# Writing out the loops of a fused state-space and codebook kernel, and finding the best code with two maxima

## The reference

```python
x = x + mamba(group_norm(x))     # layer norm, projection to 2 x 1024, causal convolution of 4 taps,
                                 # silu, selective scan with 16 states, gate, projection to 512
xf = group_norm(x)               # tokens x 512
xn = xf / norm(xf);  mn = m / norm(m)            # m: 1024 codes x 512
score = xn @ mn.T                                # 8192 x 1024
idx = argmax(score, axis=1)
counts = segment_sum(ones, idx);  esum = segment_sum(xf, idx)
new_m = m * 0.999 + esum / (counts[:, None] + 1e-6) * 0.001
x = x + softmax(score, axis=1) @ new_m
```

## Time and profile before

| | before |
|---|---|
| median of 3 runs | 4800.43 us (4799.78 to 4807.43) |
| span of the profiled execution | 4805.1 us |
| TensorE busy | 4532.6 us, 94% |
| VectorE busy | 4100.0 us, 85% |
| ScalarE, GpSimd busy | 2967.6 us, 3361.6 us |

### The profile page before, as it was taken

How to read it: one execution, slowest core, us unless ns; L and a number is a source line. 1 busy time by engine, 2 the same in 40 slices (tenths; PEclk the granted TensorE clock), 3 DMA queues, 4 the chain that set the end, 5 groups by cost and what they waited for, 6 DMA issues and landing times. The chain is left out here.

```text
span 4805.1 us, 115630 instructions
## 1 busy us (share of the span) xinstructions
PE 4532.6 (94%) x47164; PEld 2985.2 (62%) x47164; DVE 4100.0 (85%) x4361; ACT 2967.6 (62%) x6018; POOL 3361.6 (70%) x1679
## 2 busy tenths in 40 slices
PE   6999899995899999999999999999999899999999
PEld 5666666663455555555555555555554688888787
DVE  6888898877999999999999999999997667777332
ACT  2666666665777777777777777777765445453211
POOL 0666676664999999999999999999997222222000
PEclk9999999997999999999999999999999999999999
DMA  4345434335233323332333323332332111111543
GB/s 170 134 157 176 159 129 152 130 143 177 71 100 101 101 80 101 98 98 86 93 98 98 98 86 99 103 99 81 99 100 80 68 55 77 79 79 79 201 201 140
DMA packets 195543, 538.02 MB, mean 112 GB/s; under 512 B 15904, under 2 KB 15920, under 8 KB 186016
## 3 DMA queue, kind: packets, MB, share of 16 engines
q1 hardware_dynamic: 190144, 482.41, 30.4%
q0 software_dynamic: 4960, 49.25, 2.6%
HBM read 329.22 MB, written 202.38 MB: 111 GB/s over the span
## 5 line engine op out<-in xcount | busy, mean ns | idle before, releaser
L1040 POOL TENSOR_TENSOR sc_hc<-sc_hc,sc_c_rep 128x1024 f32<-128x1024 f32 x1024 | 2387.6, 2374 | 124.5 <-ACT sc_state L1053 94.7
L1235 DVE TENSOR_TENSOR_SCAN sc_hc<-l_m,sc_state,sc_ring 128x512 f32<-128x512 f32 x2048 | 2419.1, 1257 | 11.7 <-PE sc_ring L1162 7.1
L1085 ACT ACTIVATE l_m<-l1s_v,l_neg_a 128x512 f32<-128x512 f32 x2048 | 1351.4, 707 | 8.0 <-DMA l1s_v<-spill 7.7
L1162 PEld LDWEIGHTS sc_ring<-sc_diag,l1s_iota 64*64 64x64 f32 x32768 | 896.4, 133 | 459.4 <-issue 453.4
L1162 PE MATMUL sc_ring<-sc_diag,l1s_iota 64*64 64x128 f32 x32768 | 1040.8, 274 | 45.9 <-DVE sc_hc L1235 42.9
L1172 PE MATMUL sc_y_ps<-sc_hc,sc_fold 128*64 128x512 f32 x4096 | 935.4, 599 | 0.9 <-POOL sc_hc L1040 0.9
L1053 ACT ACTIVATE sc_state<-sc_hc 128x2 f32<-128x2 f32 x1024 | 207.2, 202 | 625.1 <-DVE sc_hc L1235 624.9
L1172 PEld LDWEIGHTS sc_y_ps<-sc_hc,sc_fold 128*64 128x64 f32 x4096 | 271.4, 137 | 484.0 <-issue 461.7
L1505 POOL TENSOR_TENSOR l_count<-l_count,as_oh 128x1024 f32<-128x1024 f32 x64 | 182.4, 2850 | 506.5 <-DVE as_oh L1699 506.5
L923 PE MATMUL sc_o_ps<-l_et,l_sums 128*128 128x512 f32 x960 | 464.0, 606 | 4.4 <-ACT sc_b_col L1063 4.4
L71 PE MATMUL fr_mm<-fr_xn_hi,l0f_w_in_hi 128*128 128x512 f32 x1024 | 437.0, 427 | 27.1 <-DVE fr_delta L708 11.8
(11 more groups left out here) (194 smaller groups left out, 6427.4 us busy)
## 6 DMA issues: line engine op xcount, KB each, us to landing
sc_duz<-spill SPq DMA_DIRECT2D x128, 768.0 KB, 6.0
l1s_v<-spill SPq DMA_DIRECT2D x256, 256.0 KB, 4.0
spill<-fr_z SPq DMA_DIRECT2D x64, 512.0 KB, 2.8
spill<-fr_u SPq DMA_DIRECT2D x32, 1024.0 KB, 10.0
spill<-fr_du SPq DMA_DIRECT2D x32, 1024.0 KB, 4.3
spill<-fr_delta SPq DMA_DIRECT2D x32, 1024.0 KB, 6.5
sc_c_rep<-bc SPq DMA_DIRECT2D x128, 256.0 KB, 4.5
soft<-l_et SPq DMA_DIRECT2D x16, 2048.0 KB, 6.2
```

The costliest lines, as they stand in the source:

```text
L1040: nc.gpsimd.tensor_tensor(hc[:, p], hc[:, p], c_rep[:, 2 * q:2 * q + 2, :], ALU.mult).then_inc(s_hp, 1)
L1085: nc.scalar.activation(da[:, p % 4, r, :], delta[:, i % 2, p % 2, :], ACT.Exp, scale=keep.neg_a[:, c:c + 1]).then_inc(s_da, 1)
L1162: done = nc.tensor.matmul(to[:, :, k::4], dut[rows, i % 2, k, HALF * h:HALF * h + HALF], diag[rows, u, 4 * q + c:4 * q + 4:2, k, :], start ...
L1235: nc.vector.tensor_tensor_scan(hc[:, p, r, :], da[:, p % 4, r, :], ring[:, SLOT[at], r::2], state[:, i, 2 * p + r:2 * p + r + 1], ALU.mult ...
```

## The change

The loops of `front`, `assign` and `readout` become Python loops, so that every pass is written out with constants for its waits and addresses. In `nearest` the index of the best code is found in another way: `iota` now counts down from 1024 to 1, `e` is used for a while to hold `iota` where the score equals the largest and 0 elsewhere, and a second maximum over `e` gives the highest such value, `near`. The one-hot row compares `iota` with it. `exp` waits for that second maximum, since it overwrites `e`.

```diff
-                with eng.Fori(1 - b, NJ - 1) as j:
+                for j in range(1 - b, NJ - 1):
                     main(b, j, lambda n: (b, j + n), False)
...
-                with eng.Fori(head, NJ // 2 - 1) as i:
+                for i in range(head, NJ // 2 - 1):
                     pair(b, i, False)
...
             def exp(g, s):
                 act.wait_ge(s_nb, TT * g + s + 1)
-                act.wait_ge(s_ix, TT * g + s + 1)
+                act.wait_ge(s_if, TT * g + s + 1)
...
                 dve.wait_ge(s_top, n + 1)
-                nc.vector.memset(idxf[:, s:s + 1], 0.0)
-                nc.vector.max_index(idx[:, s, :], top[:, s, :], sc_ps[:, s % 2, :]).then_inc(s_ix, 1)
+                nc.vector.memset(near[:, s, :], 0.0)
+                dve.wait_ge(s_tt, 2 * TT * g + 2 * s + 2 * TT - 2)
+                nc.vector.scalar_tensor_tensor(e[:, s % 2, :], sc_ps[:, s % 2, :], top[:, s, 0:1], keep.iota[:], ALU.is_equal,
+                                               ALU.mult).then_inc(s_ix, 1)
...
                 dve.wait_ge(s_ix, n + 1)
-                nc.vector.tensor_copy(idxf[:, s:s + 1], idx[:, s, 0:1]).then_inc(s_if, 1)
+                nc.vector.max(near[:, s, :], e[:, s % 2, :]).then_inc(s_if, 1)
...
-                nc.vector.tensor_scalar(oh[:, u, s, :], keep.iota[:], idxf[:, s:s + 1], None, ALU.is_equal).then_inc(s_oh, 1)
+                nc.vector.tensor_scalar(oh[:, u, s, :], keep.iota[:], near[:, s, 0:1], None, ALU.is_equal).then_inc(s_oh, 1)
...
-            with pool.Fori(1, NG // 2) as i:
+            for i in range(1, NG // 2):
...
-                with sp.Fori(0, NJ // 2) as i:
+                for i in range(0, NJ // 2):
...
-            with dve.Fori(0, NG // 2 - 1) as i:
+            for i in range(0, NG // 2 - 1):
...
-        "iota": np.arange(KM, dtype=np.float32)[None, :],
+        "iota": np.arange(KM, 0, -1, dtype=np.float32)[None, :],
```

More of the change, by code:

```diff
@@ L23 @@
 F32R = mybir.dt.float32r
-U32 = mybir.dt.uint32
 ALU = mybir.AluOpType
@@ L1405, in assign @@
         nb = w.sb("nb", [P, TT])
-        idx = w.sb("idx", [P, TT, 8], U32)
-        idxf = w.sb("idxf", [P, TT])
+        near = w.sb("near", [P, TT, 8])
         oh = w.sb("oh", [P, 2, TT, KM], F32R)
@@ L1779, in chunks @@
             body(1, 1, 0)
-            with eng.Fori(1, NG // 2) as i:
+            for i in range(1, NG // 2):
                 for u in range(2):
```

## The result

| | before | changed |
|---|---|---|
| median of 10 runs each, same chip | 4802.39 us (4797.68 to 4807.43) | 4816.49 us (4813.60 to 4819.77) |
| ratio, 95% interval | | 1.0025 (1.0017 to 1.0034) |
| span of the profiled execution | 4805.1 us | 4815.0 us |

The changed kernel is slower by 0.25% in the ratio (0.17 to 0.34%, 8 to 16 us), by 14.1 us in the medians and by 9.9 us in the two profiled spans. The forecast was 4818.5 us, 18.1 us more than before.

A forecast was written before the change was run, and what follows sets the result against it. TensorE was taken as the engine to watch in readout, assignment and front, counting its pauses. Terms 16.2 + 4.2 + 1.2 - 1.5 - 2.0 = +18.1 us on 4800.43 gave 4818.5 us, range 4812 to 4826.

The forecast's parts named there:

- one rival of 0.12: In `nearest`, the second maximum out of SBUF is cheap, near 0.75 us; total +9.5 us, 4810; chance 0.12.
- The steady heads: Assignment, heads of chunks 2 to 15: longer index search delays TensorE by 1.16 us at each of 14, +16.2 us.
- The other chain ends later and decides.: Assignment heads: the chain through one-hot row and `as_v_lo` to the scores, shifted 1.16 us, sets TensorE's delay.
- The prediction's bound for that chain: Assignment heads: exponential shifts about 1.2 us; `turn_tokens` takes what exceeds the copy's 0.15 us slack, about 1 us.
- Steps 0 to 2: Assignment, steady chunks: 1.2 us more on VectorE per step, not needed by TensorE at once; no cost, otherwise 58 us.
- Chunk 0 and the tail: Assignment's first chunk and last softmax: TensorE waits for VectorE itself, +4.2 us and +1.2 us.
- The assignment's loops and the readout: Removing separate waits saves 0.15 us at each of ten looped assignment heads, -1.5 us; readout without pauses gains 0.
- The front's loops: Front: GpSimd's restart wait shrinks 0.13 to 0.2 us in each of 13 looped chunks, -2.0 us.
- The upper bound of 1.3 us for a chunk: Front: most a looped chunk could gain, from one whose restart wait exceeded its neighbours', 17.45 against 16.15 us.
- if the front is shorter by more than 5 us: Front: one of the stated signs in the profile after that would show the prediction wrong.
- The rival of a smaller gain by written-out code: Front: written-out loops gain 0.5 to 1.4 us a chunk, ending at no measurable change; chance 0.03.
- equal waits at two heads: Assignment, chunks 3 and 4: both waited 0.25 us, inside a pass and at its head, so branch-fetch stalls gain none.

The follow-up runs named there:

- `as_v_lo` first: Changed kernel with `as_v_lo` of step 3 moved between the second maximum and the one-hot row; ratio 1.0018 to the kernel before.
- both edits: Changed kernel with the compare's product in the one-hot row's tile, so exp waits only for the compare, and `as_v_lo` ahead of the second maximum; ratio 0.9984.
- five versions: Kernel before with only the front's loop written out, for VectorE, GpSimd, SyncE, TensorE and ScalarE, or ScalarE: ratios 0.9995, 0.9999, 0.9998, 0.9982, 0.9963.

## Why the prediction was right, and where it was not

The forecast of 4818.5 us was 2.0 over the median measured, in its own range and on the right side. That closeness is partly luck. The forecast change was +18.1 us and the measured one +14.1; the difference shrinks to 2.0 because the median of the kernel before rose from the 4800.43 of three runs to 4802.39 of ten. The terms that were off stand below. In its chances, one rival of 0.12 "of which half ends within 0.2%" gives 0.70 + 0.10 + 0.06 = 0.86 for slower and 0.09 for the same, not 0.84 and 0.11.

- **The steady heads.** Right in mechanism, 16.2 us forecast, 13.5 shown by two pairs of kernels (with and without loops). Of the 1.16 us of shift 0.10 did not come: 0.03 from the compare (1273 ns, not 1.30 us) and 0.07 because it starts 1.28 us behind MAX8's start (3861.09 to 3862.37), where FIND_INDEX8 started 1.35 behind it, after a small operation of its own that the compare doesn't have:

```profile
3907.60 0.09 DVE L1684 MATCH_VALUE_LOAD as_idx<-as_top,as_sc_ps 128x8 f32 x1
```

  Most of what else is missing lies behind the scores: from their start to the MAX8 of the next step 3 it takes 36.84 us, 0.07 less than with the old index.
- **"The other chain ends later and decides."** True by 0.27 us only. The run with `as_v_lo` first gained 3.4 us over 14 heads and the one with both edits 15.8. Read as "`as_v_lo` is what to shorten", the sentence would have led to an edit worth a quarter of a microsecond a head. The prediction's bound for that chain, about 1 us of shift, was near: 6.64 - 5.71 = 0.93.
- **Steps 0 to 2.** Right: TensorE has no other waits there, and with both edits, where VectorE still has the long search in each step, chunks 1 to 15 take less than with the old index.
- **Chunk 0 and the tail.** 5.2 and 1.1 us in the profiles where 4.2 and 1.2 were forecast; the run with the index alone had 45.65 us in chunk 0, 4.5 more than before. The 4.2 is near for partly wrong reasons. TensorE's waits for the first softmax, for the third and at the head of chunk 1 grew to 5.13, 1.37 and 4.60 us, by 1.07, 1.04 and 1.19, 3.3 together; 1.75, 1.25 and 1.16 were forecast. The term mis-sized is the first. The table load did move by 1.66 us, from 2.63 behind MAX8's start to 4.29, but the scaling of that softmax behind it took 0.87 us instead of 1.46, which the prediction did not have. What fills the gap is the clock, which the prediction left out of chunk 0. Between the first and the second turned softmax TensorE waits in neither kernel, and the stretch takes 9.13 us (8.88 with the index alone) instead of 7.75. In the changed kernel, then in the kernel before:

```profile
3755.32:3764.45 9.13, 9.13 (x32) 7.60 (x33) 6.75 (x8) 5.08 (x8) 2.39 (x1) 0.68 0.00 1
```

```profile
3761.93:3769.68 7.75, 7.75 (x32) 6.61 (x33) 5.84 (x9) 5.08 (x8) 2.41 (x1) 0.82 0.00 0
```

  The granted clock is 0.68 instead of 0.82, that is, more of it was at 1.2 instead of 2.4 GHz behind the longer wait. Another 0.56 us lies ahead of the first wait, where the index plays no part: up to the second turning of tokens (3743.69 and 3751.36 us) the changed kernel took 12.07 us and the one before 11.51, and over all the profiles it is 11.5 to 12.3, so I count it as spread. Windows of 40 us from the middle of chunk 0 on, in the changed kernel (with a head of a steady chunk below it) and then in the kernel before, show 0.83 and 0.91. The steady head kept 1.00 behind its wait of 1.27 us.

```profile
3751.00:3791.00 40.00, 29.71 (x131) 24.64 (x132) 29.12 (x40) 20.09 (x34) 11.46 (x4) 0.83 0.07 24
3866.00:3876.00 10.00, 9.07 (x47) 7.59 (x48) 6.39 (x8) 5.31 (x15) 4.16 (x1) 1.00 0.05 7
```

```profile
3759.00:3799.00 40.00, 33.32 (x155) 27.44 (x156) 30.13 (x51) 22.34 (x38) 13.68 (x5) 0.91 0.16 60
```
- **The assignment's loops and the readout.** 1.4 us (1.5 forecast) and 0.2.
- **The front's loops: the step that failed.** "So 0.13 to 0.2 us for each of 13 looped chunks: 13 x 0.15 = -2.0 us." I compared the waits at GpSimd's restart in looped and written-out chunks of one profile, and they do differ by no more. The wait isn't the whole period: in the long form GpSimd's own 32 operations carried another 0.9 us of stretching, which no comparison of waits shows, and the written-out chunk of the second image stood among chunks in that form. Where both kernels are in the short form, the looped chunk costs 0.3 us more, which is near the term. The upper bound of 1.3 us for a chunk was taken from one more fall of the clock, which was another thing. By the ratios the front's loop gave 6 us (2 to 11) where 2.0 was forecast, and all the loops 9 us (5 to 13) where 3.5 was; in the two profiles the front gave 9.7. By my own sign, "if the front is shorter by more than 5 us", this part was wrong in the profiles. The rival of a smaller gain by written-out code, at 0.5 to 1.4 us a chunk and a chance of 0.03, has the size that the profiles show (9.7 / 13 = 0.75; by the ratio 0.5), but neither its end, since the kernel did get measurably slower, nor its mechanism: the idle times of TensorE and ScalarE in a whole chunk of the short form differ by 0.2 us between the two kernels (pauses over 0.1 us from 338.74 to 403.65 and from 338.82 to 403.41 us: 4.67 and 4.51, 22.62 and 22.43), which leaves no room for a stall at a loop's end beyond that. Nor do equal waits at two heads refute what the prediction takes from the Trainium skill, "Runtime: NRT & Kernel Launch", section on instruction fetch mechanics, since no run here shows whether a branch of these loops leaves the resident pages.
- **The sum.** Index +19.7 by its own run (13 to 26 by the interval, 17.2 by the medians) against +21.6 forecast; loops -9 (-13 to -5) against -3.5. Together 10.7 from the two runs; the pair has 12 by the ratio and 14.1 by the medians, well within these intervals. An index term that was too high and a gain of the loops that was put too small both make the forecast change too large, which it was by 4 us in the medians.

**Open.** That writing out ScalarE's loop is what shortens the front is shown by the times of five versions. That it does so by keeping the long form out rests on single profiled executions. Why it would is only argued: ScalarE has most of the open waits of the cycle, and each separate wait may delay a restart by something like the 0.15 us seen at the assignment's heads, enough to change who comes first at the shared port. No run moved VectorE's operations against GpSimd's directly. Whether TensorE's loop does harm when written out (ratio 0.9982 with it, 0.9963 without it, on different sets of runs) is open too. The 1.4 us by which the scan was longer in the changed kernel's profile (2589.2 and 2587.8 us from TensorE's first work in it to chunk 0) I count as spread: the other profiles lie between 2586.9 and 2589.4.

## What to carry to other kernels

When two chains release an engine within a fraction of a microsecond, a longer step on a shared part of them costs nearly in full, and a shorter step on one of them gives at most the distance between them (here 0.27 us): move both or neither. Before adding an operation to an engine that is awaited, look for what waits behind it without needing it: here `as_v_lo` and the exponential, and with both moved ahead the longer search cost nothing that the times show. The gain of written-out code can't be read from the written-out chunks of a looped program; compare whole periods, and the durations of single operations, not only the wait at one place.

## What the runs showed of the hardware

- A MAX8 over 1024 columns takes 1223 ns out of SBUF and 1226 out of PSUM; a compare and multiply of that size with one input in PSUM takes 1273. Two operations of the 512-column form out of SBUF would take 2 x 756 = 1512.
- `fr_r`, VectorE's operation of 2048 columns, takes 1.23 us when it starts first and 2.32 when GpSimd does; GpSimd's of 512 columns takes 1.3 alone and 2.33 beside it. A front chunk took 65.60 us with the first order and 64.58 with the second at the same clock, and with the same looped program the order differed within one execution and between two.
- Writing out all loops raised the instruction fetches from 337 packets and 5.52 MB to 376 and 6.16 MB; no wait was traced to them.
